# Five even blocks for the row maxima of an attention kernel (460 or 462 columns in place of 256 and four of 512)

## The chip, the cores and the metric

The kernel runs on one core of a Trainium2 chip. The metric is the device time of one execution in microseconds. The kernel before takes 6809.67 us (median of 3 runs, 6804.43 to 6810.84).

## The reference

Four layers, each on two images of 48 x 48 pixels with 192 channels: group norm (32 groups), then self-attention with 12 heads of 16 channels and relative positions, then a projection, added to the input:

```python
attn = einsum('bqc,bkc->bqk', q * scale, k)            # 2304 x 2304 per image and head
attn = attn + rel_h[..., :, None] + rel_w[..., None, :]
attn = softmax(attn, axis=-1)
out  = attn @ v                                         # then @ proj_w + proj_b, and x + ...
```

In all 4 x 2 x 12 = 96 units (a unit is one head of one image in one layer), each with 2304 queries and 2304 keys. The softmax needs the largest score of each query before the exponentials.

## The kernel before, in words

A stage is one image of one layer (8 stages), a stage has 12 heads, a head is a unit `u`. A unit has 18 tiles `t` of 128. The kernel computes every score twice.

First, for the maxima, with 128 queries on the partitions and keys along the columns: `hi` (the queries with their position terms) is the stationary operand, `mkeys` the moving one, in float32r. The 2304 keys of a tile are cut into the five blocks of `MSPLIT`; the product of a block (line 805) goes into one of the three PSUM banks `aux`, and VectorE reduces it to one number per query (line 683, into `mpart`). When all 18 tiles of a unit are done, VectorE takes the maximum over the five parts (line 725), TensorE turns the result into a row (`mt`, line 830), and ACT copies it to `mrow`, which enters the second computation as one more row of the contraction.

Second, for the scores, with 128 keys on the partitions and queries along the columns: `keys` is stationary, `moving` the moving operand; the five blocks of `SPLIT` (four of 512, the last of 256) go into the three PSUM banks `score` (line 796), and ACT writes their exponentials to `probs` (line 561). One tile later TensorE multiplies `probs` with the values (line 878, in float32, eight products in 16 rows) and gathers the sums over all keys.

The order of all this is written out by hand in `schedule()`. For every unit and tile there are six places `i` = 0 to 5. At place `i` < 5 TensorE does the plan's items, among them one maximum block, and then one score block; at place 5 it does the sums of the tile before (`attend`). So a tile on TensorE reads m0, s0, m1, s1, m2, s2, m3, s3, m4, s4, sums. The maxima run KEEP = 4 tiles more than a unit ahead of the scores. Further items: `rel` (line 824, the position products, at the start of tiles 0 to 11; ACT copies them out, lines 544 and 549, and VectorE rounds them to `hi`, line 721, in tiles 8 to 13), `qk` (line 843, projections for the next stage, in every second tile of heads 4 to 6, ahead of s3), `v` (line 851, heads 7 and 8) and `fin` (line 862, heads 1 and 2), both right behind m0, and `gn` (line 835, head 3). In head 3 of a stage VectorE also does the group norm of the next: in tiles 0 to 5 one BATCH_NORM_STATS2 (line 633) at place 1, ahead of m1's reduction, and one at place 3; later small steps linked by a semaphore. At places 0 and 1 of tile 1 ACT also copies out the sums of the unit before (line 590).

Banks are taken in turn. Every item that VectorE reads uses the next `aux` bank, every item that ACT reads the next `score` bank; before it TensorE waits until the item three places back in that turn has been read. That wait sits on the weight load (LDWEIGHTS). So m3 waits for the reduction of m0, and m4 for that of m1; s3 and s4 in the same way for the exponentials of s0 and s1.

The lines around the change:

```python
SPLIT = [(512 * i, min(512 * i + 512, N)) for i in range(5)]
SB = len(SPLIT)
MSPLIT = SPLIT[-1:] + SPLIT[:-1]      # (2048, 2304), (0, 512), (512, 1024), (1024, 1536), (1536, 2048)
...
lo, up = MSPLIT[m]                                                        # fill(), TensorE
pe.matmul(bank[:, 0:up - lo], hi[:, u % 2, q * P:(q + 1) * P], mkeys[:, u % 2, lo:up], ...)
...
dve.tensor_reduce(mpart[:, u % 2, q, m:m + 1], bank[:, 0:MSPLIT[m][1] - MSPLIT[m][0]], AX.X, ALU.max)
```

Of the kernel before, what the change touches and what calls it, by code (L numbers as in the profile page):

```python
# [15 lines left out]
N = SIDE * SIDE  # L16
# [21 lines left out]

SPLIT = [(512 * i, min(512 * i + 512, N)) for i in range(5)]
SB = len(SPLIT)  # L40
MSPLIT = SPLIT[-1:] + SPLIT[:-1]
MT_AT = 2

QK_AT = 1
# [74 lines left out]
def build(nc, a):  # L119
# [3 lines left out]
    with ExitStack() as ctx:  # L123
# [482 lines left out]
        def _(dve):  # L606
# [70 lines left out]
            def consume(item):  # L677
# [3 lines left out]
                if item[0] == "max":  # L681
                    _, u, q, m = item
                    dve.tensor_reduce(mpart[:, u % 2, q, m:m + 1], bank[:, 0:MSPLIT[m][1] - MSPLIT[m][0]], AX.X, ALU.max)\  # L683
                        .then_inc(dve_read, 1)
# [83 lines left out]
        def _(pe):  # L768
# [14 lines left out]
            def fill(item):  # L783
# [14 lines left out]
                elif item[0] == "max":  # L798
                    _, u, q, m = item
                    lo, up = MSPLIT[m]  # L800
                    if m == 0 and q % 3 == 0:
# [152 lines left out]
```

## Time and profile before

| what | value |
|---|---|
| median of 3 runs | 6809.67 us |
| span of the profiled execution, first to last instruction | 6801.4 us |
| runs' median less that span | 8.3 us |
| TensorE matmuls (PE) busy | 6725.5 us, 99% |
| VectorE (DVE) busy | 5454.7 us, 80% |
| ScalarE (ACT) busy | 4753.7 us, 70% |
| GpSimd (POOL) busy | 938.1 us, 14% |
| mean granted TensorE clock | 0.996 |

The profile has no time of its own for what lies around the span; the difference of 8.3 us holds that and the difference between executions. The ends of matmuls are modelled, so starts are the better measure: the time that a matmul takes from the others is that from its start to the next start. PE is a matmul, PEld the load of its stationary operand, which may run beside the matmul before. A reduction's row is longer than the step to the next one, because consecutive instructions overlap.

### The profile page before, as it was taken

Reading aid. Unit: us, or ns where it says so; the run is one execution under the profiler, and the core shown is the slowest. Engines: PE = TensorE matmul, PEld = TensorE weight load, DVE = VectorE, ACT = ScalarE, POOL = GpSimd, SP = SyncE. Lnnn points to the kernel's source line nnn. Section 1 sums busy time; section 2 is a strip of 40 time slices with the busy share of each in tenths; the row PEclk is TensorE's granted clock in tenths of the full one; section 3 lists DMA queues with packets and bytes.
Section 4 is the critical chain, followed back from the end, with each engine's and each line's share of the span. In section 5 each row is a group of like instructions: output and inputs, shape, how many; then the busy total and the mean of one; then the engine's idle time right before and its main releaser. Section 6 shows DMA issues by size and latency. Waiting matters only on the chain.

```text
span 6801.4 us, 139326 instructions
## 1 busy us (share of the span) xinstructions
PE 6725.5 (99%) x53600; PEld 4245.8 (62%) x53600; DVE 5454.7 (80%) x9973; ACT 4753.7 (70%) x10225; POOL 938.1 (14%) x967
## 2 busy tenths in 40 slices
PE   7999999999999999999999999999999999999998
PEld 5666666666666666666665666666666666666664
DVE  7887888778887788877888778887888878888883
ACT  3776776767767777677776767767676676767775
POOL 2111010211112110121111210102101121101110
PEclk8999999999999999999999999999999999999999
DMA  6676676767677677667676766767677676777673
GB/s 164 148 156 152 137 160 138 163 151 142 152 144 168 144 143 156 149 158 149 142 155 149 158 143 143 161 145 166 140 144 157 147 165 138 143 152 156 144 154 88
DMA packets 306307, 1013.72 MB, mean 149 GB/s; under 512 B 107440, under 2 KB 196976, under 8 KB 215920
## 3 DMA queue, kind: packets, MB, share of 16 engines
q1 hardware_dynamic: 305648, 1004.81, 68.9%
q8 instruction: 429, 7.03, 0.5%
q14 instruction: 230, 1.88, 0.1%
HBM read 745.26 MB, written 255.69 MB: 147 GB/s over the span
## 4 chain that ended last, share of the span: by engine, by line
PE 96%; DMA 1%; DVE 1%; issue 0%; ACT 0%; SPq 0%; POOL 0%; DVEq 0%; ACTq 0%
PE work L805 30%; PE work L878 27%; PE work L796 27%; PE work L824 7%; PE work L843 3%; PE work L862 2%; PE work L851 1%; DMA moving<-rel_scratch 1%; DVE mpart L683 1%; PE work L830 0%; DVE xb L674 0%; ACT probs L561 0%; DMA back<-attention_scratch 0%; DVE hi L721 0%; PE work L835 0%
## 5 line engine op out<-in xcount | busy, mean ns | idle before, releaser
L683 DVE TENSOR_REDUCE mpart<-work 128x1 f32<-128x512 f32 (+1 forms) x8640 | 5088.7, 632 | 1079.7 <-PE work L805 1013.1
L561 ACT ACTIVATE probs<-work 128x512 f32<-128x512 f32 (+1 forms) x8640 | 4100.2, 564 | 866.6 <-PE work L796 852.1
L805 PE MATMUL work<-mkeys,hi 128*128 128x512 f32 (+1 forms) x8640 | 3404.1, 395 | 10.6 <-DVE mpart L683 8.8
L796 PE MATMUL work<-moving,keys 113*128 113x512 f32 (+1 forms) x8640 | 3299.9, 383 | 10.9 <-DMA moving<-rel_scratch 5.7
L805 PEld LDWEIGHTS work<-mkeys,hi 128*128 128x128 f32 x8640 | 1643.6, 190 | 622.4 <-DVE mpart L683 324.0
L878 PE MATMUL work<-probs,vall 128*17 128x288 f32 x27648 | 2013.1, 409 | 0.0
L796 PEld LDWEIGHTS work<-moving,keys 113*128 113x128 f32 x8640 | 1642.1, 190 | 362.3 <-ACT probs L561 39.2
L878 PEld LDWEIGHTS work<-probs,vall 128*17 128x17 f32 x27648 | 637.3, 96 | 846.8 <-ACT probs L561 358.3
L824 PEld LDWEIGHTS work<-image,tab 128*48 128x48 f32 x6912 | 401.6, 124 | 544.9 <-ACT probs L561 513.2
L490 POOL TENSOR_TENSOR full<-full,hi 128x384 f32<-128x384 f32 x576 | 583.5, 1016 | 938.7 <-DVE hi L721 937.6
L495 POOL TENSOR_TENSOR rden<-oraw,rden 128x576 f32<-128x576 f32 x96 | 137.1, 1428 | 3955.3 <-DMA rden<-inverse_scratch 3955.3
L549 ACT ACTIVATE full<-work 48x384 f32<-48x384 f32 x576 | 279.3, 485 | 514.1 <-PE work L824 513.3
L544 ACT ACTIVATE full<-work 48x384 f32<-48x384 f32 x576 | 279.2, 486 | 454.4 <-PE work L824 454.4
L824 PE MATMUL work<-image,tab 128*48 128x48 f32 (+1 forms) x6912 | 532.6, 211 | 4.9 <-DMA image<-qk_scratch 4.9
L721 DVE CAST hi<-full 128x384 fp32r<-128x384 f32 x576 | 243.1, 423 | 10.2 <-ACT full L549 9.2
L843 PE MATMUL work<-xb,wqk 96*128 96x384 f32 x576 | 211.5, 489 | 6.7 <-DVE xb L674 6.7
L503 POOL CAST split_hi<-back 128x384 fp32r<-128x384 f32 x144 | 75.6, 525 | 923.3 <-ACT back L583 915.8
L583 ACT ACTIVATE back<-work,bqks,qkscale 128x384 f32<-128x384 f32 x144 | 96.7, 672 | 132.5 <-PE work L843 132.5
L862 PE MATMUL work<-back,wproj 96*96 96x384 f32 x384 | 140.9, 493 | 16.9 <-issue 15.8
L505 POOL TENSOR_TENSOR back<-back,split_hi 128x384 f32<-128x384 f32 x144 | 146.0, 1014 | 11.5
L843 PEld LDWEIGHTS work<-xb,wqk 96*128 96x128 f32 x576 | 109.9, 191 | 57.4 <-DVE xb L674 6.8
L690 DVE SCALAR_TENSOR_TENSOR xb<-work,bproj,xb 96x384 f32<-96x384 f32 x96 | 58.9, 613 | 98.3 <-PE work L862 98.3
(42 smaller groups left out, 646.8 us busy)
## 6 DMA issues: line engine op xcount, KB each, us to landing
moving<-rel_scratch SPq DMA_DIRECT2D x1728, 144.0 KB
moving<-qk_scratch SPq DMA_DIRECT2D x288, 576.0 KB
rel_scratch<-hi SPq DMA_DIRECT2D x192, 432.0 KB, 5.7
rel_scratch<-full SPq DMA_DIRECT2D x192, 432.0 KB, 5.5
moving<-rel_scratch SPq DMA_DIRECT2D x288, 288.0 KB
image<-qk_scratch SPq DMA_DIRECT2D x384, 144.0 KB, 3.2
keys<-qk_scratch SPq DMA_DIRECT2D x192, 288.0 KB, 7.8
qk_scratch<-split_hi SPq DMA_DIRECT2D x144, 192.0 KB, 3.9
```

The costliest lines, as they stand in the source:

```text
L490: pool.tensor_tensor(full[:, cols], full[:, cols], hi[:, u % 2, cols].bitcast(F32), ALU.subtract)\
L544: act.activation(to, bank[0:SIDE, 0:BLK].rearrange("p (x n) -> p x n", x=NB), ACT.Copy)\
L549: act.activation(to, bank[0:SIDE, 0:BLK].rearrange("p (w h) -> p h w", w=8), ACT.Copy)\
L561: act.activation(probs[:, tile % RING, lo:up], bank[:, 0:up - lo], ACT.Exp).then_inc(act_read, 1)
L683: dve.tensor_reduce(mpart[:, u % 2, q, m:m + 1], bank[:, 0:MSPLIT[m][1] - MSPLIT[m][0]], AX.X, ALU.max)\
L721: dve.tensor_copy(hi[:, u % 2, cols], full[:, cols]).then_inc(hi_ready, 1)
L796: pe.matmul(bank[:, 0:up - lo], tile_of(keys[0:K_ROWS, u % 2, :], c, third), moving[0:K_ROWS, slot_of(u, third)[0], lo:up], start=True, st ...
L805: pe.matmul(bank[:, 0:up - lo], hi[:, u % 2, q * P:(q + 1) * P], mkeys[:, u % 2, lo:up], start=True, stop=True).then_inc(for_dve, 1)
L824: mm = pe.matmul(to, tab[:, layer, d, SIDE - 1 - at:2 * SIDE - 1 - at], query, start=True, stop=True)
L843: mm = pe.matmul(bank[:, 0:BLK], wqk[:, t, m * P:(m + 1) * P], xb[:, t, g * BLK:(g + 1) * BLK], start=(t == 0), stop=(t == 1))
L862: mm = pe.matmul(bank[0:HALF, 0:BLK], wproj[:, t, m * HALF:(m + 1) * HALF], aob[:, k % 2, t, :], start=(t == 0), stop=(t == 1))
L878: mm = pe.matmul(sums[32 * j:32 * j + VCOL, part, 0:QCOL], vall[:, b * QT + t, h, :], probs[:, tile % RING, at:at + QCOL], start=(t == 0), ...
```

## The change

The maxima get blocks of their own, of 462, 462, 460, 460 and 460 columns, in the order of the keys. The scores keep four of 512 and then 256.

```diff
 SPLIT = [(512 * i, min(512 * i + 512, N)) for i in range(5)]
 SB = len(SPLIT)
-MSPLIT = SPLIT[-1:] + SPLIT[:-1]
+EDGES = [0, 462, 924, 1384, 1844, N]
+MSPLIT = list(zip(EDGES[:-1], EDGES[1:]))
 MT_AT = 2
```

Nothing else differs: the number of products and reductions, the order of the items and all waits are the same.

## Rows read from the trace of the kernel before

**Rows 1.** The page: busy time of each engine; the chain that ended last, by engine
```profile
PE 6725.5 (99%) x53600; PEld 4245.8 (62%) x53600; DVE 5454.7 (80%) x9973; ACT 4753.7 (70%) x10225; POOL 938.1 (14%) x967
...
PE 96%; DMA 1%; DVE 1%; issue 0%; ACT 0%; SPq 0%; POOL 0%; DVEq 0%; ACTq 0%
```

**Rows 2.** Groups by line and shape: count, busy us, mean ns of one, idle before
```profile
L683 DVE TENSOR_REDUCE mpart<-work 128x1 f32<-128x512 f32 x6912 | 4367.1, 683 | 188.9 <-PE work L805 128.5
...
L805 PE MATMUL work<-mkeys,hi 128*128 128x512 f32 x6912 | 2770.3, 402 | 10.4 <-DVE mpart L683 8.8
...
L683 DVE TENSOR_REDUCE mpart<-work 128x1 f32<-128x256 f32 x1728 | 732.0, 424 | 890.9 <-PE work L805 884.6
...
L805 PE MATMUL work<-mkeys,hi 128*128 128x256 f32 x1728 | 635.4, 368 | 0.2
```

**Rows 3.** Timeline, TensorE, an ordinary tile: start us, duration us, what
```profile
3505.92 0.39 PE L805 MATMUL work<-mkeys,hi 128*128 128x256 f32 x1
3506.02 0.19 PEld L796 LDWEIGHTS work<-moving,keys 113*128 113x128 f32 x1
3506.14 0.39 PE L796 MATMUL work<-moving,keys 113*128 113x512 f32 x1
...
3507.55 0.40 PE L796 MATMUL work<-moving,keys 113*128 113x512 f32 x1
3507.55 0.19 PEld L805 LDWEIGHTS work<-mkeys,hi 128*128 128x128 f32 x1
3507.78 0.40 PE L805 MATMUL work<-mkeys,hi 128*128 128x512 f32 x1
...
3508.01 0.28 PE L796 MATMUL work<-moving,keys 113*128 113x256 f32 x1
3508.22 1.17 PE L878 MATMUL work<-probs,vall 128*17 128x288 f32 x16
```

**Rows 4.** Timeline, VectorE, the same tile: the reductions of m0, m1 and m2
```profile
3506.34 0.42 DVE L683 TENSOR_REDUCE mpart<-work 128x1 f32<-128x256 f32 x1 [0.18 <-PE work L805]
...
3506.80 0.69 DVE L683 TENSOR_REDUCE mpart<-work 128x1 f32<-128x512 f32 x1
...
3507.41 0.68 DVE L683 TENSOR_REDUCE mpart<-work 128x1 f32<-128x512 f32 x1
```

**Rows 5.** Timeline, TensorE, tile 15 of a head 3: s3, load of m4, m4
```profile
2059.63 0.39 PE L796 MATMUL work<-moving,keys 113*128 113x512 f32 x1
...
2059.75 0.19 PEld L805 LDWEIGHTS work<-mkeys,hi 128*128 128x128 f32 x1 [0.16 <-DVE mpart L683]
...
2059.86 0.39 PE L805 MATMUL work<-mkeys,hi 128*128 128x512 f32 x1
```

**Rows 6.** Timeline, VectorE and TensorE, tile 0 of head 3, to the next m0
```profile
2000.00 0.35 PE L805 MATMUL work<-mkeys,hi 128*128 128x256 f32 x1
...
2000.39 0.42 DVE L683 TENSOR_REDUCE mpart<-work 128x1 f32<-128x256 f32 x1 [0.59 <-PE work L805]
...
2000.73 0.55 DVE L633 BATCH_NORM_STATS2 stats<-xb 96x6 f32<-96x384 f32 x1
...
2001.20 0.67 DVE L683 TENSOR_REDUCE mpart<-work 128x1 f32<-128x512 f32 x1
...
2001.59 0.39 PE L796 MATMUL work<-moving,keys 113*128 113x512 f32 x1
...
2001.92 0.19 PEld L805 LDWEIGHTS work<-mkeys,hi 128*128 128x128 f32 x1 [0.37 <-DVE mpart L683]
...
2003.79 0.35 PE L805 MATMUL work<-mkeys,hi 128*128 128x256 f32 x1
```

**Rows 7.** Timeline, TensorE and ACT, tile 1 of a head 9: s0, its exponential, load for s4
```profile
2433.04 0.40 PE L796 MATMUL work<-moving,keys 113*128 113x512 f32 x1
...
2433.47 0.60 ACT L561 ACTIVATE probs<-work 128x512 f32<-128x512 f32 x1
...
2434.91 0.19 PEld L796 LDWEIGHTS work<-moving,keys 113*128 113x128 f32 x1 [0.27 <-ACT probs L561]
```

## The prediction

> **What bounds the kernel now.** I read the table of engines first: TensorE's matmuls fill 6725.5 us of the 6801.4 us span, VectorE 5454.7 us [rows 1]. The chain that ended last says the same, 96% of it TensorE work [rows 1]. So every added nanosecond on TensorE counts, and an engine behind it counts only where it holds TensorE up. The groups by line and shape name the work that the change touches: 1728 tiles of maxima, each with one product of 256 columns and four of 512 (L805), and as many reductions on VectorE (L683) [rows 2]. Last I read the timeline of single tiles of 128 queries. One tile on TensorE is: m0, s0, m1, s1, ... m4, s4 (a maximum block and a score block by turns), then the 16 rows of the sums (L878), then in 12 of 18 tiles the small products of L824. In [rows 3] the reader is to see that nothing in this row waits: from m0 at 3505.92 to the sums at 3508.22 a start comes every 0.23 us.
>
> **The matmuls themselves: 0.** A 512 block takes (3508.01 - 3506.14) / 8 = 0.234 us from start to start [rows 3]. m0 of 256 columns stands 0.22 us before s0, but about 0.105 of that is the load of its own weights, which nothing hides behind the sums (the load for s0 begins 0.10 us after m0's stamp): leaves 0.117. The slope is (0.234 - 0.117) / 256 = 0.457 ns a column. The stamped durations, 0.28 against 0.39 us [rows 3], give 0.43 to 0.46. On this line a block of 460 or 462 costs 0.210 us. A tile before: 4 x 0.234 + 0.117 = 1.053 us; after: 2304 x 0.457 ns = 1.053 us. Same number of products, same columns: any cost of the form fixed + slope x columns cancels. No row shows a block between 256 and 512, so I bound it. Above: 460 columns cost what 512 do, +0.117 us a tile, x 1706 tiles that also hold scores = +200 us. Below: 460 columns at one column per cycle of the 2.4 GHz level at which it runs here would be 0.192, -0.09 us a tile; what then follows is a rival below. I take 0, because two sizes and two kinds of reading (starts, durations) lie on one line.
>
> **VectorE's sum: 0 too.** Reductions that don't wait follow each other at 0.60 us for 512 columns (3506.80 to 3507.41) [rows 4] though one lasts 0.68. A 256 one lasts 0.42 [rows 2, 4], so a column costs (0.68 - 0.42) / 256 = 1.0 ns; 460 take 0.63 and follow at 0.545. Per tile 4 x 0.60 + 0.34 = 2.74 before, 5 x 0.545 = 2.73 after, where a tile takes 6801.4 / 1728 = 3.9 us on average. The engine isn't the bound in most tiles.
>
> **What moves is the order in time.** The first block becomes the long one. With m0's stamp as zero, s0 and m1 start 0.093 us later (204 x 0.457 ns), and every later maximum block gives 0.024 back: s1 and m2 +0.07, s2 and m3 +0.045, s3 and m4 +0.02, sums 0. The readers behind do not get it back as fast:
> - VectorE before: m0 read from 0.42, m1 from 0.88 to 1.57 (3506.80 + 0.69) [rows 4]; the weight load of m4, which needs m1's bank (three banks, taken in turn), follows 0.05 later at 1.63, just at s3's stamp [rows 3]. After: m0 from 0.515, m1 from 0.515 + 0.545 = 1.06 to 1.69, load of m4 at 1.74. s3 now stands at 1.65 and m4 at 1.885. So the load comes 0.09 us after s3's stamp and not with it.
> - Is that late? The tile of [rows 5] shows a load of m4 0.12 us behind s3, waiting for VectorE (0.16 idle), and m4 only 0.23 us behind s3: no loss. A load needs about 0.11 us of lead, so it may come 0.12 late. The slack of an ordinary tile shrinks from about 0.12 to 0.03 us, the loss is 0. The page "TensorE: Matmul & The Clock Gate" of the Trainium skill, Part 3 (What overlaps and what doesn't), says that a weight load overlaps a running matmul only where it uses another row group. By that rule a load that comes 0.09 late costs 0.09 in each tile; the load in rows 5 is one of all 128 rows and was hidden, so here the trace does not agree.
> - ACT: s0's exponential starts 0.09 later. In an ordinary tile s4 (which needs s1's bank) has room, as m4's load has.
>
> **Where there is no room.** (1) In head 3 of seven stages, tiles 0 to 5, VectorE also does two BATCH_NORM_STATS2, the first between m0 and m1. Before: m0 2000.39, statistics 2000.73, m1 2001.20 to 2001.87, load of m4 at 2001.92 after 0.37 us idle, where 2001.82 or so would have been m4's start [rows 6]; TensorE already waits 0.2 us per tile. After: m0 +0.093, statistics and m1 another +0.20 (the 204 columns more in m0's read, less a pause of 0.01 that stood there), m1's read 0.054 shorter: load of m4 +0.24. m4 itself is 0.024 shorter. +0.22 us x 42 tiles = +9.2 us. (2) In the same unit the group sums and scales are chained on VectorE between the reductions in tile 6 and tiles 9 to 12; the same mechanism in 5 x 7 tiles, but there VectorE is partly bound by its unchanged sum, so I take +2 us between 0 and 35 x 0.22 = 7.7. (3) In tile 1 of each head ACT also takes out the sums of the head before (L590), after s0 and after s1. There the load for s4 waits 0.27 us for ACT [rows 7]. ACT starts on s0 at 2433.47, which is s0's stamp 2433.04 + 0.40 + 0.04: with s0 0.093 later everything up to s1's read is 0.093 later, and s4 and the sums with it. 95 such tiles, less 21 where a projection product of 1.3 us lies ahead of s3 and hides it, less 7 that are in (1): 67 x 0.093 = +6.2 us, between 0 (if ACT's copy of L824's result, which comes just before, set that start alone) and 95 x 0.093 = 8.8.
> Tiles with an output or value product after m0 (heads 1, 2, 7, 8) pause VectorE there, and it starts m1 anew: 0. Transfers are issued on the score blocks' counts, which end where they did: 0.
>
> **Sum.** 9.2 + 2 + 6.2 = +17.4 us on the profiled 6801.4: 6818.8. The median of the runs shown is 8.3 us above that span (what lies around it, and other executions); it becomes 6827.
>
> **Rivals.**
> - Faster: 460 columns cost less than the line says, because 512 pay something extra. For it: 512 blocks come at 0.234 where 512 cycles at 2.4 GHz are 0.213, so there is an extra, and where between 256 and 512 it begins no row shows. Against: the two points have it in proportion. VectorE caps the gain: the load of m4 can't come before 1.74, m4 starts at 1.85, sums 0.41 later at 2.26 against 2.30 before: -0.04 x 1700 = -68, plus 17: 6760 at best. It decides from a block cost of about 0.208 down.
> - Slower than forecast: the slack of 0.03 us is not there (reads of 460 that follow at 0.56 rather than 0.545, or bank releases a little later). 0.03 us over in every tile is +51 us: 6878. In full, a late load that is never hidden: +0.09 x 1706 = +154: 6981 (it is also what the quoted rule would give). It decides once m4's load is more than 0.12 behind s3. For it: the slack is the smallest in the kernel. Against: the hidden load of [rows 5].
> - Nothing: terms (1) and (3) are swallowed by pauses that the timeline doesn't let me see, and the time stays at 6810. Against it: both places show TensorE's loads idle for exactly these engines [rows 6, 7].
> - That the change does nothing at all is excluded: widths of both product and reduction come from the list that is replaced.
>
> **How the numbers follow.** Forecast 0.55, own range 6815 to 6845; cheaper columns 0.18; slack gone 0.12 (in full 0.04); nothing 0.15. A change under 0.2% (13.6 us) can't be told from none. The forecast's +17 is close to that: of its 0.55, 0.41 is slower and 0.14 same. Cheaper columns: 0.16 faster, 0.02 same. Slack gone: slower. Nothing: 0.11 same, 0.03 faster, 0.01 slower. Together faster 0.19, same 0.27, slower 0.54. Range 6762 to 6880: it leaves out the full rival above and the upper bound of the block's cost.
>
> **What would show it.** Right: in an ordinary tile s0 0.31 to 0.32 us behind m0 where it was 0.22, s1 0.21 behind m1, sums 2.30 behind m0; reductions of 0.63 that follow at 0.545; the load of m4 0.09 behind s3 with m4 still 0.23 behind s3. In head 3, tiles 0 to 5, 4.01 us from m0 to m0 where [rows 6] have 3.79; in tile 1 of most heads the load for s4 idles 0.36 us, not 0.27. Wrong: a start-to-start after a maximum block clearly off 0.210, or m4 late in every tile.

## The result and the profile after

The changed kernel takes 6843.61 us (median of 5 runs, 6841.53 to 6845.02) against 6808.41 us (5 runs) of the kernel before: ratio 1.0052, 95% interval 1.0040 to 1.0064. It is slower by 35 us where 17 were forecast (6827, from 6809.67). Single runs of one kernel lie up to 18 us apart, so a difference of a few us between medians is read from the traces. The profiled execution has a span of 6839.7 us, 38.3 more than the one before.

The page of the changed kernel, its table of engines and its chain by engine, answers to [rows 1]:
```profile
PE 6759.6 (99%) x53600; PEld 4316.6 (63%) x53600; DVE 5330.0 (78%) x9973; ACT 4793.7 (70%) x10225; POOL 938.2 (14%) x967
...
PE 94%; DVE 3%; DMA 2%; issue 0%; ACT 0%; SPq 0%; POOL 0%; DVEq 0%; ACTq 0%
```
TensorE is as full as before, VectorE's share of the chain has gone from 1 to 3%, that of the transfers from 1 to 2%. The change adds one line to the program, so line 805 of before is 806 here, 683 is 684, and so on. The groups by line and shape (count, busy us, mean ns of one, idle before) answer to [rows 2]:
```profile
L684 DVE TENSOR_REDUCE mpart<-work 128x1 f32<-128x460 f32 x5184 | 3028.0, 627 | 116.0 <-PE work L806 115.8
L684 DVE TENSOR_REDUCE mpart<-work 128x1 f32<-128x462 f32 x3456 | 2063.1, 633 | 1153.4 <-PE work L806 1144.8
...
L806 PE MATMUL work<-mkeys,hi 128*128 128x460 f32 x5184 | 1973.0, 382 | 11.7 <-DVE mpart L684 6.6
...
L806 PE MATMUL work<-mkeys,hi 128*128 128x462 f32 x3456 | 1446.4, 419 | 1.5 <-DVE mpart L684 1.1
```
A reduction of 460 lasts 0.627 us where the forecast had 0.63. The timeline of an ordinary tile (tile 12 of a head 0), TensorE's matmuls, answers to [rows 3]:
```profile
3525.86 0.48 PE L806 MATMUL work<-mkeys,hi 128*128 128x462 f32 x1
3526.18 0.40 PE L797 MATMUL work<-moving,keys 113*128 113x512 f32 x1
3526.42 0.38 PE L806 MATMUL work<-mkeys,hi 128*128 128x462 f32 x1
3526.63 0.40 PE L797 MATMUL work<-moving,keys 113*128 113x512 f32 x1
...
3527.53 0.40 PE L797 MATMUL work<-moving,keys 113*128 113x512 f32 x1
3527.77 0.37 PE L806 MATMUL work<-mkeys,hi 128*128 128x460 f32 x1
3527.98 0.28 PE L797 MATMUL work<-moving,keys 113*128 113x256 f32 x1
3528.19 0.44 PE L879 MATMUL work<-probs,vall 128*17 128x288 f32 x4
```
and its weight load for m4:
```profile
3527.62 0.19 PEld L806 LDWEIGHTS work<-mkeys,hi 128*128 128x128 f32 x1
```
s0 stands 0.32 us behind m0 (forecast 0.31 to 0.32), s1 0.21 behind m1, the load of m4 0.09 behind s3, all as worked out, and m4 0.24 behind s3 (forecast 0.23). But the sums stand 2.33 behind m0 and not 2.30. Tile 0 of head 3, VectorE and TensorE, answers to [rows 6]:
```profile
2010.27 0.64 DVE L684 TENSOR_REDUCE mpart<-work 128x1 f32<-128x462 f32 x1 [0.79 <-PE work L806]
2010.82 0.55 DVE L634 BATCH_NORM_STATS2 stats<-xb 96x6 f32<-96x384 f32 x1
2011.29 1.16 DVE L684 TENSOR_REDUCE mpart<-work 128x1 f32<-128x462 f32 x2
```
```profile
2009.79 0.44 PE L806 MATMUL work<-mkeys,hi 128*128 128x462 f32 x1
...
2011.41 0.40 PE L797 MATMUL work<-moving,keys 113*128 113x512 f32 x1
2011.96 0.48 PE L806 MATMUL work<-mkeys,hi 128*128 128x460 f32 x1 [0.15 <-DVE mpart L684]
...
2013.81 0.44 PE L806 MATMUL work<-mkeys,hi 128*128 128x462 f32 x1
```
s3 to m4 is 0.55 us, it was 0.33; the tile takes 4.02 us for 3.79. Tile 1 of head 9, the load for s4, answers to [rows 7]:
```profile
2448.15 0.19 PEld L797 LDWEIGHTS work<-moving,keys 113*128 113x128 f32 x1 [0.25 <-ACT probs L562]
```
It idles 0.25 us, about as before (the forecast had 0.36), because the load ahead of it, that of m4, is now late too and idle time counts from its end; what tells is that it comes 2.16 us behind m0 (2446.00) and no longer 2.06.

**Where the 38 us are.** Each tile's time (first score matmul to the next tile's first, the last one to the end), summed in each trace and subtracted:

| tiles | forecast | measured |
|---|---|---|
| head 3 of seven stages, tiles 0 to 5 (42) | +9.2 us | +9.6 us |
| head 3, its other tiles (84) | +2 | +2.5 |
| tile 1 of the other heads (88) | +6.2 | +6.5 |
| all others (1514) | 0 | +20.7, a mean of 13.7 ns |

These add up to 39.3 us; the stretch ahead of the first score matmul is 1.0 us shorter. The order in time did what was said. The term that was taken as 0 is more than half of the loss. The next table has the steps from start to start in ns, for the change and the later experiments. Each is a mean over the 1352 tiles in which no other product stands between these blocks, of the steps under 260 ns (m0-s0 under 330), so without those that waited. The step m0-s0 is 0.22 us in the tile of [rows 3], but shorter in tiles 0 to 11, where products of L824 stand ahead of m0 (2000.00 to 2000.19 in tile 0 of head 3, before); so the sum of the means is under the 2.30 us of that tile.

```
                       m0-s0 s0-m1 m1-s1 s1-m2 m2-s2 s2-m3 m3-s3 s3-m4 m4-s4 s4-sums | sum
before                 201.8 234.7 233.0 234.7 235.4 235.1 234.8 232.8 233.3 209.0  | 2284.6
changed                294.8 235.2 212.8 236.8 213.6 236.7 212.6 236.9 210.1 209.7  | 2299.2
short reads            294.6 234.8 212.8 236.8 213.1 237.3 213.3 232.8 208.7 212.5  | 2296.7
460 x4, 464            294.3 235.1 210.3 234.2 209.2 238.6 208.2 231.3 213.1 210.2  | 2284.5
460 x3, 462 x2         294.4 235.0 210.2 234.0 209.3 238.7 209.6 231.7 212.6 210.5  | 2286.0
462 at aligned starts  294.9 234.8 212.3 234.5 210.3 233.8 213.1 232.7 215.4 209.9  | 2291.7
460 at off starts      294.0 234.8 213.4 232.8 212.1 236.4 212.5 232.3 214.0 210.0  | 2292.2
464, 456 (32 bytes)    295.9 235.9 212.4 233.8 207.9 236.9 209.8 236.7 213.8 209.5  | 2292.5
258, 512 at off starts 202.8 236.3 234.3 234.1 232.4 232.9 232.0 232.5 233.7 210.7  | 2281.7
```

Changed less before is 14.6 ns: +5.6 behind the maximum blocks, +9.0 behind the score blocks, whose widths the change does not touch. The traces of experiments 1 to 3, which have the change's blocks too, give sums of 2299.0 to 2299.9, and experiments 11 and 12 give 2286.8 for 460 x4, 464 and 2285.0 for the blocks of before: one way to cut comes out within 2.3 ns of itself.

### The profile page after: what moved, and what is told of

It is laid out like the page before. It is cut to its first block, busy times and chain, and to the rows that moved or that the text cites. A ratio compares the mean times of both kernels' runs of the same rounds, so it can differ in the third digit from the quotient of the medians.

```text
span 6839.7 us, 139326 instructions
## 1 busy us (share of the span) xinstructions
PE 6759.6 (99%) x53600; PEld 4316.6 (63%) x53600; DVE 5330.0 (78%) x9973; ACT 4793.7 (70%) x10225; POOL 938.2 (14%) x967
## 4 chain that ended last, share of the span: by engine, by line
PE 94%; DVE 3%; DMA 2%; issue 0%; ACT 0%; SPq 0%; POOL 0%; DVEq 0%; ACTq 0%
PE work L806 29%; PE work L879 27%; PE work L797 26%; PE work L825 6%; PE work L844 3%; DVE mpart L684 2%; PE work L863 2%; PE work L852 1%; DMA moving<-rel_scratch 1%; PE work L831 0%; DVE xb L675 0%; DVE stats L634 0%; DMA back<-attention_scratch 0%; ACT probs L562 0%; DVE hi L722 0%
## 5 line engine op out<-in xcount | busy, mean ns | idle before, releaser
L684 DVE TENSOR_REDUCE mpart<-work 128x1 f32<-128x460 f32 (+1 forms) x8640 | 4954.3, 629 | 1269.4 <-PE work L806 1260.6
L806 PE MATMUL work<-mkeys,hi 128*128 128x460 f32 (+1 forms) x8640 | 3416.3, 397 | 13.2 <-DVE mpart L684 7.7
```

## The experiments

The times are medians of 4 to 11 runs; beside them the kernel before took 6809.4 to 6809.8 us (medians of 17 to 28 runs, single ones 6799.7 to 6818.1). The 95% interval of a ratio to it is about 0.1% (7 us) to either side. Three theories of the loss: A, the order of the readers (VectorE and ACT late); B, the matmul itself off the straight line between 256 and 512 columns; C, later called S, where in `mkeys` a block starts. In experiments 6 and 7 a fourth is W: a width that is no multiple of four columns costs.

**1. Statistics one place later (on the change).**
```diff
-                            if i in (1, 3) and t < NB:
-                                last = stat(s + 1, 2 * t + i // 2)
+                            if i in (2, 4) and t < NB:
+                                last = stat(s + 1, 2 * t + i // 2 - 1)
```


> The kernel with even blocks, with the two BATCH_NORM_STATS2 of tiles 0 to 5 of head 3 one place later each (before m2's and m4's reduction, not m1's and m3's). Theory A (the loss in these tiles is m0's longer read plus the statistics ahead of m1, which delays m4's weight load): VectorE's own sum of about 3.66 us becomes the bound, the tiles go from 4.01 to about 3.66 us, 42 x 0.35 = -14.7 us: about 6829. Rival (these tiles are bound by VectorE's sum whatever the order): they stay at 4.01 and the time at 6844.

Measured 6830.4 us, -13. Tiles 0 to 5 of head 3 gave 14.7 us back. Timeline of tile 2 of head 3, TensorE (from m0 through s3 and m4 to the next m0):
```profile
2014.04 0.44 PE L806 MATMUL work<-mkeys,hi 128*128 128x462 f32 x1
...
2015.66 0.40 PE L797 MATMUL work<-moving,keys 113*128 113x512 f32 x1
2015.90 0.38 PE L806 MATMUL work<-mkeys,hi 128*128 128x460 f32 x1
...
2017.64 0.44 PE L806 MATMUL work<-mkeys,hi 128*128 128x462 f32 x1
```
m4 is 0.24 behind s3 again, and the tile takes 3.60 us, less than VectorE's sum of 3.66. So VectorE falls behind: m0's reduction starts 0.48 us behind m0 in tile 0 and 0.98 behind it in tile 6 (means over the seven heads), and tiles 6 and 10 pay 4.4 us later. Theory A holds for these tiles; the rival is out.

**2. A copy of the sums on VectorE: the wrong half.** ACT's copies at places 0 and 1 of tile 1 are `sums_out(u - 1, 0)` after s0 and `sums_out(u - 1, 1)` after s1. Here the second goes to VectorE, ahead of m0's reduction.
```diff
-                        if t == 1 and i < 2 and 1 <= u <= UNITS:
-                            sums_out(u - 1, i)
+                        if t == 1 and i == 0 and 1 <= u <= UNITS:
+                            sums_out(u - 1, 0)
...
+                        if t == 1 and i == 0 and 1 <= u <= UNITS:   # VectorE: tensor_copy
+                            sums_out(u - 1, 1)
```


> The kernel with even blocks, with the second half of the head's sums copied out by VectorE at the start of tile 1, ahead of m0's reduction, and the first half by ACT as now. Theory A (in tile 1 the load for s4 waits for ACT, which is 0.09 us later than with the small first block): ACT's chain is 0.29 us shorter, the wait goes, tile 1 falls from 3.785 to 3.60 us in the 74 heads without a projection product, -14 us: about 6830. Rival (tile 1 is late for another reason, as the sums' own wait for the copy): no change, 6844, or slower by VectorE's later m0, 95 x 0.05 = +5 us.

Measured 6843.3 us: a miss. ACT in tile 1 of head 9, then the load for s4 (the eight lines inserted move the score product from line 797 to 805 here and in experiment 3):
```profile
2449.10 0.60 ACT L562 ACTIVATE probs<-work 128x512 f32<-128x512 f32 x1
2449.60 0.41 ACT L591 ACTIVATE oraw<-work 128x288 f32<-128x288 f32 x1
2449.89 1.86 ACT L562 ACTIVATE probs<-work 128x512 f32<-128x512 f32 x4
```
```profile
2450.54 0.19 PEld L805 LDWEIGHTS work<-moving,keys 113*128 113x128 f32 x1 [0.25 <-ACT probs L562]
```
s4 needs the bank of s1, so only what ACT does ahead of s1's exponential counts, and that copy (2449.60) is the first half's.

**3. The right half.** The same with the halves exchanged: the first by VectorE at place 0, the second by ACT after s1 (`i == 1`).

> The kernel with even blocks (462, 462, 460, 460, 460), with the first half of the head's sums copied out by VectorE at the start of tile 1 and the second half by ACT after s1. The run with the second half on VectorE showed no change, and its trace has ACT's copy of the first half between s0's and s1's exponentials, where it delays the bank that s4 needs. Theory A: with that copy gone s1 is read 0.29 us sooner, the load for s4 no longer waits, tile 1 falls from 3.785 to about 3.60 us in 67 to 74 heads: 6844 - 13 = about 6831. Rival (tile 1 waits for the sums' copies themselves): no change, 6844.

Measured 6828.4 us, -15. The same two views of tile 1 of head 9 (m0 at 2442.67):
```profile
2443.38 1.09 ACT L562 ACTIVATE probs<-work 128x512 f32<-128x512 f32 x2
2444.35 0.42 ACT L591 ACTIVATE oraw<-work 128x288 f32<-128x288 f32 x1
2444.64 1.38 ACT L562 ACTIVATE probs<-work 128x512 f32<-128x512 f32 x3
```
```profile
2444.53 0.19 PEld L805 LDWEIGHTS work<-moving,keys 113*128 113x128 f32 x1
```
The load for s4 comes 1.86 us behind m0 instead of 2.16 and waits for nobody. Summed over all the tiles 1, that is -12.7 us. The third term of the forecast has its cause: s0 and with it ACT, late by m0's extra width.

**4. Short reads.** Each reduction reads 256 columns, so the maxima leave out the rest and the result is not that of the reference.
```diff
-bank[:, 0:MSPLIT[m][1] - MSPLIT[m][0]], AX.X
+bank[:, 0:256], AX.X
```


> The kernel with even blocks whose reductions read the first 256 columns of each block only, so the maxima leave out the other columns; every product is as it was. VectorE is never late: the load of m4 stands at s3's stamp, the tiles 0 to 5 of head 3 lose their 0.42 us. Theory A (the regular +10 ns of an ordinary tile come from the late load of m4 and the order of the reads): an ordinary tile falls back from 2.318 to about 2.306 us from m0 to the sums, 6843 - 17 - 18 = about 6808. Theory B (a product of 460 costs TensorE itself 2 to 3 ns more than the line from 256 to 512 says): only the head 3 tiles fall, ordinary tiles stay near 2.315, about 6825.

Measured 6802.6 us, -41. The span of the profiled execution is 45.6 us shorter. Of that, 11.1 us lie ahead of the first score matmul, where only maxima are computed and a tile comes every 1.82 us instead of 2.72. 33.7 us lie in head 3: its waits for VectorE are gone, those that the kernel before has too. The 1514 ordinary tiles give back 1 us in all. An ordinary tile, TensorE, and its load of m4:
```profile
3496.92 0.48 PE L806 MATMUL work<-mkeys,hi 128*128 128x462 f32 x1
...
3498.58 0.40 PE L797 MATMUL work<-moving,keys 113*128 113x512 f32 x1
...
3499.24 0.44 PE L879 MATMUL work<-probs,vall 128*17 128x288 f32 x4
```
```profile
3498.58 0.19 PEld L806 LDWEIGHTS work<-mkeys,hi 128*128 128x128 f32 x1
```
The load stands at s3's stamp, yet m0 to the sums is still 2.32 us. In the table s3 to m4 gives back 4.1 ns and the two steps behind it lose 1.4; all ten steps together give back 2.5 ns of 14.6. For the ordinary tiles VectorE's part in theory A is out. ACT's part, which this run leaves as it was, falls with experiment 5, where ACT starts as late and the loss is gone.

**5. Blocks that start at multiples of 16 bytes.**
```diff
-EDGES = [0, 462, 924, 1384, 1844, N]
+EDGES = [0, 460, 920, 1380, 1840, N]
```


> Blocks of 460, 460, 460, 460, 464 columns, so each starts at a multiple of 16 bytes in mkeys; before, m1 started at byte 1848. Theory C (a block that starts within a 16 byte line is read more slowly): s1 to s1's predecessor m1 falls from 0.212 to about 0.210 us, -2 ns x 1700 = -3 us or more. Theories A and B: no change beyond noise, 6844, m4 to s4 0.002 longer and m0 0.001 shorter.

Measured 6823.2 us, -20, where theory C had 3 or more. An ordinary tile (its first and last matmul):
```profile
3514.87 0.48 PE L806 MATMUL work<-mkeys,hi 128*128 128x460 f32 x1
...
3517.17 0.44 PE L879 MATMUL work<-probs,vall 128*17 128x288 f32 x4
```
2.30 us, as before the change, with the same five blocks to within 4 columns. By the table the sum is 2284.5 against 2284.6 ns. So even blocks need not cost more on TensorE. Theory B, as a cost of the width alone, is out as well: experiment 8 below has the change's own widths and a sum of 2286.0. What remains of this kernel's loss is the late readers: 14 us by the medians, and in the trace 9.5 us in tiles 0 to 5 of head 3, 2.0 in its others and 6.3 in the tiles 1, with 3.7 in all the rest.

**6 and 7. Start or width?** `MSPLIT` with overlapping blocks (a column that is seen twice doesn't change a maximum).
```diff
+MSPLIT = [(0,462),(460,922),(920,1382),(1380,1842),(1840,2304)]      # 6: starts aligned, widths 462
+MSPLIT = [(0,460),(458,918),(918,1378),(1378,1838),(1838,2304)]      # 7: starts 8 bytes off, widths 460
```


> Blocks that start at 0, 460, 920, 1380, 1840 (multiples of 16 bytes) but hold 462, 462, 462, 462, 464 columns, two of them twice at each seam; the maxima are the same. Theory S (the start of a block within 16 bytes costs): as the kernel with 460s at the same starts, 6823, plus 8 columns x 0.457 ns x 1728 = +6: about 6829. Theory W (a width that is no multiple of four columns costs): every block is now such a width, so 6843 or above, about 6850 to 6860.

> Blocks of 460 columns (the last 466) that start at 0, 458, 918, 1378 and 1838: all four later starts lie 8 bytes off a multiple of 16. Theory S: four blocks pay where the kernel with 462 and 460 had one so far off, so it is at least as slow as that, 6844 plus up to 10. Theory W: only the last block has such a width: about 6823 plus 2 columns, 6825 to 6830.

Measured 6831.0 and 6831.4 us. The first fits theory S and rules out W. The second does not fit S: four starts off cost 8 us over the aligned kernel (about 1.6 of it for two more columns, an estimate at 0.457 ns a column) where one start off, in the change, had cost 20.

**8 and 9. The same widths reversed, and large blocks at off starts.**
```diff
+EDGES = [0, 460, 920, 1380, 1842, N]                                  # 8, on the change
+MSPLIT = [(0, 258), (258, 770), (770, 1282), (1282, 1794), (1794, N)] # 9, on the kernel before
```


> The same five widths as in the change, the other way round: 460, 460, 460, 462, 462, starts 0, 460, 920, 1380, 1842, only the last one off a multiple of 16 bytes. Theory S, and the two runs so far that lie at 6831 with all starts on or off: one off start costs a quarter of four, 6823 to 6828. Rival (any 462 among them costs as in the change): 6843.

> Blocks of 258, 512, 512, 512, 510 that start at 0, 258, 770, 1282, 1794: all four large ones lie 8 bytes off a multiple of 16. Columns and widths are as good as those of the kernel before. Theory S (an off start costs about 1 to 3 ns a block): +4 to +12 ns a tile, 6816 to 6830. Rival (starts as such cost nothing; it is the pattern of widths and times of the even kernel): 6809.

Measured 6827.1 us (8) and 6803.2 us, ratio 0.9994, interval 0.9985 to 1.0003 (9). The first is within what theory S had (6823 to 6828): the same five widths the other way round, with other starts, are worth 16 us. The second is not (6816 to 6830): four large blocks 8 bytes off cost nothing, and theory S, as a price per block, falls.

**10. Multiples of 32 bytes.** `EDGES = [0, 464, 928, 1384, 1840, N]`.

> Blocks of 464, 464, 456, 456, 464 columns, so each starts at a multiple of 32 bytes, each width a multiple of 8. If finer alignment than 16 bytes pays further: ordinary tiles under 2.300 us from m0 to the sums, 6815 or less. If 16 bytes are all there is to it: as with 460, 460, 460, 460, 464, 6823.

Measured 6833.4 us, which neither expectation had: finer alignment doesn't help, it is 10 us over the kernel of 5. The sums of the table run from 2284.5 to 2299.2 ns over six ways to cut the row into five nearly even blocks (two of them with overlaps), and no property of start or width that I tried orders them. The traces show one thing more. The steps do not spread about their mean; they lie in groups, and the cut moves how often each comes. From m2 to s2, 460 columns in both kernels, the step is under 208 ns in 487 of 1352 tiles of experiment 5 and in none of the change; from s2 to m3, 512 columns, it is 240 to 243 in 254 tiles of the kernel before, 398 of the change and 852 of experiment 5.

**11 and 12. A better version.** Both edits (1 and 3) on the aligned even blocks, and on the kernel before.

> Blocks of 460, 460, 460, 460, 464 with the statistics of head 3 one place later and the first half of the sums copied by VectorE. If the three parts add: 6823 - 13 (statistics) - 13 (copy) = about 6797, under the kernel before (6810) by 0.2%. If they share a cause: 6810 or more.

> The kernel before (256 and four of 512) with the statistics of head 3 one place later and the first half of the sums copied out by VectorE. Theory A: both waits are there with the small first block too, only shorter (0.2 us in 42 tiles, 0.11 us in 67 or more): 42 x 0.125 = 5 and 74 x 0.11 = 8, so 6809 - 13 = about 6796, a little under the same two edits with blocks of 460 and 464 (6803). Rival (the two edits only take back what even blocks had lost): 6809.

Measured 6803.5 us (ratio 0.9989, 0.9980 to 0.9999) and 6802.6 us (0.9987, 0.9978 to 0.9996). Both beat the kernel before by about 0.1%, with intervals that end just below 1; which blocks are used no longer matters. On the even blocks the two edits gave 20 us, not the 26 of the sum. On the kernel before the edits were worth 7 us and not 13: in tile 1 they gave 6.7, in tiles 0 to 5 of head 3 3.9, but tile 6 there took 3.1 back, as VectorE's backlog came due.

## Why the prediction was right, and where it was not

- **"Matmuls themselves: 0"** is the term that failed. It measured a mean of +13.7 ns in 1514 tiles, +20.7 us. The straight line comes out for one cut, that of experiment 5 (a sum of steps of 2284.5 ns against 2284.6), and the other five even cuts of the table lie 1.4 to 14.6 ns above before, that of the change the most: the steps of ordinary tiles depend on how exactly the row is cut, and 9 of the 14.6 ns stand behind score blocks, to which the forecast's sum gave no cost at all. The bounds (-0.09 to +0.117 us a tile) held it; the value taken did not.
- **VectorE's sum: 0.** Right. Reductions of 460 last 0.627 us and follow each other at 0.544 (the median of those with nothing between), where the forecast had 0.63 and 0.545.
- **The late load of m4 costs nothing.** It comes 0.09 late in ordinary tiles, as worked out. Without the lateness (experiment 4) the steps of the table give 2.5 ns back, whole ordinary tiles 1 us in all 1514. Right; the slack of 0.03 us was enough, and the rival that had it used up did not come about. The page "TensorE: Matmul & The Clock Gate" of the Trainium skill (Part 3, What overlaps and what doesn't) has a weight load overlap a running matmul only where the two use different row groups, so not this load of all 128 rows. The trace of the changed kernel doesn't agree: the load lasts 0.19 us, starts 0.09 behind s3, and m4 starts 0.24 behind s3.
- **(1) Statistics:** 9.6 for 9.2 us, 0.23 a tile for 0.22, and experiment 1 shows the cause by moving them.
- **(2) The rest of head 3:** 2.5 for 2 us. Its cause was not tested alone, and 84 tiles at the ordinary 13.7 ns would be 1.2 of it, so that it came close is in part luck.
- **(3) ACT in tile 1:** 6.5 for 6.2 us: 0.08 to 0.11 us in nearly all of them, and under 0.03 in heads 4 to 6 of seven stages, where a projection product hides it, as forecast. The cause is shown by experiments 2 and 3 together: of two copies only the one ahead of s1's exponential counts. The sign that was named for it, 0.36 us of idle time before the load for s4, did not show (0.25): it left out that m4's load, ahead of it, comes 0.09 later too.
- **Transfers: 0.** TensorE's matmuls and loads waited 19.5 us for transfers before and 20.6 after, so their waits account for about 1 us. Single tiles differ between the two profiled executions by up to 2 us in both directions; I did not follow them.
- **The faster rival** (columns cheaper than the line) had its block cost at 0.208 or below; in experiment 5 it is 0.208 to 0.213 and the tile is even with before. It did not happen.

The time, 6844, is just inside the forecast's own range (6815 to 6845), and that is luck: by the traces 19 us come from the late readers, as forecast, and 21 from a term set to 0, for a reason that the forecast did not have.

What stays open is why the cut matters. Starts, widths and their order were varied; neither the distance to 16 or 32 bytes nor a width off a multiple of four explains the six sums. That the cut sets them is shown by experiments 5 and 8; by what path is not. A run that shifts the score blocks' times without touching the maxima would be a next step; none was made.

## What to carry to other kernels

When two engines work through a short ring of buffers, the width of the first block of a burst sets when every reader starts. Here its extra width came back as 16 us in places that had no slack, though no sum had changed, so the small block belongs first as long as such places are there; once they were mended (experiments 11 and 12) it no longer mattered. Look for the places where a reader does something else between the first and the second block (here the statistics and a copy), and move that behind the block whose buffer is needed next. And a zero that rests on a straight line through two sizes is an estimate: it needs a range of its own. Here it came out at 21 us.

## What the runs showed of the hardware that I had not expected

- A tile with the same 2304 columns in five instructions takes 2284.5, 2286.0, 2292.5 or 2299.2 ns, by cuts whose blocks differ by 2 to 8 columns. Part of the difference shows behind matmuls that were not changed: over all rows of the table the five score steps add up to 1146 to 1155 ns, the five maximum steps of the six even cuts to 1135 to 1146.
- In the kernel before, a float32r matmul of 512 columns with its own weights comes every 0.233 to 0.235 us (means of the table) at a granted clock of 0.996 of 2.4 GHz, where 512 cycles are 0.213; in the even cuts 460 columns come every 0.208 to 0.214.
- A weight load that starts 0.10 us behind the previous matmul's stamp (460 x4, 464: s3 3516.52, load 3516.62, m4 3516.75) leaves that step at 231.3 ns, the shortest behind a score block of 512 in the table.
